# The last mixture of a graph kernel: 32 lists of one expert, or 8 lists of four

## The reference, cut to what matters

```python
    xf = x.reshape(-1, D)                       # 8192 x 128, layer-normed
    logits = xf @ router_w.T + router_b         # E = 32
    idx = jnp.argmax(logits, axis=-1)
    h = jnp.einsum('nd,ndh->nh', xf, jnp.take(W1, idx, axis=0)) + jnp.take(b1, idx, axis=0)   # H = 32
    h = jax.nn.relu(h)
    out = jnp.einsum('nh,nhd->nd', h, jnp.take(W2, idx, axis=0)) + jnp.take(b2, idx, axis=0)
    out = jax.nn.relu(out)
    ...
x = x + _L3_ffn_ref(_layernorm(x, axis=-1), ...)
```

## Time and profile before

| | us |
|---|---|
| median of three runs | 1954.38 |
| lowest and highest run | 1948.59, 1958.46 |
| span of the profiled execution | 1867.1 |
| TensorE busy | 1627.8 (87%) |
| VectorE busy | 1095.9 (59%) |
| ScalarE busy | 998.9 (53%) |
| GpSimd busy | 786.7 (42%) |

### The profile page before, as it was taken

The page is one execution under the profiler, slowest core; times in us unless marked ns, Lnnn a source line. Parts: engine busy times, 40 slices in busy tenths (PEclk is TensorE's granted clock), DMA queues, the critical chain, the costliest instruction groups (busy, mean ns, idle before and its releaser), DMA issues. The chain is left out here.

```text
span 1867.1 us, 43356 instructions
## 1 busy us (share of the span) xinstructions
PE 1627.8 (87%) x13366; PEld 1314.2 (70%) x13366; DVE 1095.9 (59%) x4199; ACT 998.9 (53%) x3116; POOL 786.7 (42%) x1358
## 2 busy tenths in 40 slices
PE   7978899988859987999998888879999888884995
PEld 5756677767759985788887566679999845553542
DVE  7933433348737777699998755523333377763552
ACT  5854444446636656666665433246666534441663
POOL 6710000014426666111111677745565434554675
PEclk9989999999969999899999799989999989995998
DMA  3200000010014420000000511122222253105331
GB/s 114 84 1 1 1 1 1 1 27 1 1 36 134 123 80 1 2 3 2 2 3 3 156 47 48 62 62 70 72 71 72 56 150 86 58 24 88 100 86 35
DMA packets 125926, 91.76 MB, mean 49 GB/s; under 512 B 23591, under 2 KB 116554, under 8 KB 125701
## 3 DMA queue, kind: packets, MB, share of 16 engines
q1 hardware_dynamic: 109110, 61.89, 12.6%
q0 software_dynamic: 13568, 25.90, 4.3%
q10 hardware_dynamic: 3024, 1.21, 0.4%
HBM read 57.71 MB, written 33.30 MB: 49 GB/s over the span
## 5 line engine op out<-in xcount | busy, mean ns | idle before, releaser
L1361 ACT ACTIVATE FEAT<-BANKS,FEAT 128x128 f32<-128x128 f32 x544 | 155.5, 368 | 82.1 <-PE BANKS L1314 82.1
L1206 POOL DMA_INDIRECT scratch_made<-FEAT x136 | 144.9, 1065 | 122.6 <-DVE FEAT L1500 119.8
L1061 ACT ACTIVATE EXP<-BANKS,NEGMAX 128x128 f32<-128x128 f32 x512 | 139.4, 383 | 59.5 <-DVE NEGMAX L1073 59.5
L440 ACT ACTIVATE gates<-BANKS,EXP 128x64 f32<-128x64 f32 x384 | 97.4, 314 | 112.6 <-PE BANKS L417 112.6
L1314 PE MATMUL BANKS<-FEAT 128*128 128x128 f32 x1088 | 145.5, 277 | 0.0
L1323 PE MATMUL BANKS<-AUX,FEAT 128*128 x1088 | 144.5, 276 | 0.4 <-ACT FEAT L1361 0.4
L417 PEld LDWEIGHTS BANKS<-AUX,EXP 128*128 128x128 f32 x768 | 95.4, 191 | 69.7 <-DVE AUX L464 69.6
L1198 POOL DMA_INDIRECT scratch_sent<-FEAT,POS x128 | 125.1, 977 | 38.3 <-issue 37.5
L990 POOL COPY EXP<-AUX 128x32 f32<-128x32 f32 x256 | 42.5, 211 | 217.8 <-PE BANKS L1036 217.8
L1314 PEld LDWEIGHTS BANKS<-FEAT 128*128 128x128 f32 x1088 | 133.9, 194 | 0.0
L1323 PEld LDWEIGHTS BANKS<-AUX,FEAT 128*128 128x128 f32 x1088 | 133.2, 193 | 0.6 <-issue 0.6
(11 more groups left out here) (367 smaller groups left out, 4196.0 us busy)
## 6 DMA issues: line engine op xcount, KB each, us to landing
EXP<-in_L_ffn_W SPq DMA_DIRECT2D x128, 128.0 KB, 2.1
FEAT<-scratch_sent SPq DMA_DIRECT2D x136, 64.5 KB
EXP<-scratch_made SPq DMA_DIRECT2D x32, 256.0 KB, 3.4
FEAT<-scratch_sent SPq DMA_DIRECT2D x96, 65.5 KB, 1.9
X<-in_x SPq DMA_DIRECT2D x16, 256.0 KB, 2.9
STAGE<-in_adj SPq DMA_DIRECT2D x16, 256.0 KB, 3.3
scratch_sent<-NONE SPq DMA_DIRECT2D x48, 65.5 KB, 3.3
scratch_sent<-FEAT,POS POOLq DMA_INDIRECT x192, 2.3
```

The source lines that it names most:

```text
L440: act.activation(gates[:, at, sp_, :], PS[2 * at + par][:, u * B:(u + 1) * B], f, bias=wr["b" + gate]).then_inc(done, 1)
L1061: last = act.activation(tile(EXS[:, par], 4 * k + n), tile(PS[j], c), ACT.Exp, bias=NEGMAX[:, par, 4 * k + n:4 * k + n + 1])
L1206: pool.indirect_dma_start(out=made2, out_offset=bass.IndirectOffsetOnAxis(ap=XI_I[:, t % R_IN, H:ROW2], axis=0), in_=YO[:, t % R_OUT, :], ...
L1361: last = act.activation(tile(HR[:, t % R_H], c), tile(PS[2 + t % 2], c), ACT.Gelu, bias=BT[:, c, t:t + 1])
```

## The change

The 32 experts are held as 8 lists of four (`L3` = 8, `M3` = 4). The list is expert // 4, and expert mod 4 travels with the token as a one-hot of four words at the front of its row (135 words instead of 131). The stream has 64 + 8 = 72 tiles, or 18 quads.

A tile now meets all four experts of its list at once. The first layer is one product over the whole array: 128 inputs to 4 x 32 hidden values. A mask product adds the bias: a one-hot column times a table `BT3` that holds b1 where expert and column agree and -2^100 elsewhere, so that relu turns the three other experts' hidden values to zero. The second layer is one product of 128 x 128 for a tile, on top of the b2 picked by the same one-hot. The one-hots of four tiles are turned by one transpose. Every stage works on a quad. There is one unread product of 256 columns a quad, where there was one a tile.

```diff
-        NT3 = B * T // P + E3
+        NT3 = B * T // P + L3
...
+                def clear(i):
+                    if i == 0:
+                        pool.memset(BT3, NEVER).then_inc(s.none, 1)
+                        pool.memset(OP3, 0.0).then_inc(s.none, 1)
+                    if i < 3:
+                        pool.memset(BR3[i], 0.0).then_inc(s.none, 1)
+                in_turn(NG, [(0, dev), (2, dev2), (2, clear), (6, send)])
...
                 def later(i):
+                    if i < L3:
+                        some = slice(M3 * i, M3 * i + M3)
+                        sp.dma_start(WT3[:, 256 * i:256 * i + P].rearrange("p (e f) -> p e f", e=M3),
+                                     a["L3_ffn_W1"][some].rearrange("e d f -> d e f")).then_inc(load_e3, 16)
+                        sp.dma_start(WT3[:, 256 * i + P:256 * i + 2 * P], a["L3_ffn_W2"][some].rearrange("e f d -> (e f) d")
+                                     ).then_inc(load_e3, 16)
...
-                for e in range(0, E3 // 2):
+                for e in range(0, L3 // 2):
                     r = sp.value_load(ZROW3[0:1, e:e + 1]).with_bounds(min_val=0, max_val=ROWS3 - P)
                     sp.dma_start(sent3[bass.ds(r, P), :], NONE3[:, e:e + ROW3]).then_inc(s.ex3_blank, 16)
...
-                in_turn(NT3, [(0, turn), (0, keep_warm), (1, up), (2, down)])
+                def turn(q):
+                    reused(pe, s.ex3_hot, q, 2)
+                    pe.wait_ge(s.ex3_xn, q + 1)
+                    pe.transpose(OB3[q % 2][:, 0:P], OP3[:, q % 2, :], ident[:])
+                    pe.matmul(OB3[q % 2][:, P:3 * P], ident[:], ident[:].unsqueeze(1).to_broadcast([P, 2, P]), start=True, stop=True)
+                    reused(pe, s.ex3_xT, q, 2)
+                    transpose4(pe, PS[q % 2], XN3[:, q % 2], s.ex3_t_ps)
+
+                def mask(q):
+                    pe.wait_ge(s.ex3_hot, q + 1)
+                    pe.wait_ge(s.ex3_w, 8 * (q + 1))
+                    reused(pe, s.ex3_hT, q, 2)
+                    reused(pe, s.ex3_y, q, 2)
+                    for j in range(4):
+                        pe.matmul(tile(PS[2 + q % 2], j), BR3[q % 3][:, j, 0:P], OT3[:, q % 2, :],
+                                  start=(j == 0), stop=False, skip_group_check=True)
+                    pe.matmul(Y3[q % 2].rearrange("p (k h) -> p k h", k=4), OT3[:, q % 2, :], BR3[q % 3][:, :, P:2 * P],
+                              start=True, stop=False, skip_group_check=True)
+
+                def up(q):
+                    pe.wait_ge(s.ex3_xT, q + 1)
+                    for j in range(4):
+                        last = pe.matmul(tile(PS[2 + q % 2], j), WR3[q % 3][:, 256 * j:256 * j + P], tile(XT3[:, q % 2], j),
+                                         start=False, stop=True, skip_group_check=True)
+                    last.then_inc(s.ex3_h_ps, 1)
+
+                def down(q):
+                    pe.wait_ge(s.ex3_hT, q + 1)
+                    for j in range(4):
+                        last = pe.matmul(tile(Y3[q % 2], j), tile(HT3[:, q % 2], j), WR3[q % 3][:, 256 * j + P:256 * j + 2 * P],
+                                         start=False, stop=True, skip_group_check=True)
+                    last.then_inc(s.ex3_y_ps, 1)
+                in_turn(NQ, [(0, turn), (1, mask), (1, up), (2, down)])
...
+                def first(q):
                     reused(act, s.ex3_y_ps, q, 3)
+                    for j in range(4):
+                        e = act.value_load(EOFI3[0:1, 4 * q + j:4 * q + j + 1]).with_bounds(min_val=0, max_val=L3 - 1)
+                        rows = slice(32 * j, 32 * j + M3)
+                        act.copy(BR3[q % 3][rows, j, :], BT3[rows, bass.ds(e * 256, 256)]).then_inc(s.ex3_w, 1)
+                        act.copy(WR3[q % 3][:, 256 * j:256 * j + 256], WT3[:, bass.ds(e * 256, 256)]).then_inc(s.ex3_w, 1)
+
+                def units(q):
+                    act.wait_ge(s.ex3_h_ps, q + 1)
+                    reused(act, s.ex3_y_ps, q, 2)
+                    act.activation(HT3[:, q % 2, :], PS[2 + q % 2], ACT.Relu).then_inc(s.ex3_hT, 1)
...
+                in_turn(NQ, [(2, units), (0, first)])
...
                     v.wait_ge(s.idx, i + 1)
+                    v.tensor_scalar(PART3[:, par, 0, :], IDX3[:].bitcast(INT32)[:, par, :, 0], 2, None, ALU.arith_shift_right)
+                    v.tensor_scalar(PART3[:, par, 1, :], IDX3[:].bitcast(INT32)[:, par, :, 0], M3 - 1, None, ALU.bitwise_and
+                                    ).then_inc(s.part, 1)
...
+                    v.tensor_tensor(OUTBOX3[:, i % R_SEND3, :, 0:M3], iota32[:, 0:M3].unsqueeze(1).to_broadcast([P, G, M3]),
+                                    PART3[:, par, 1, :].unsqueeze(2).to_broadcast([P, G, M3]), ALU.is_equal)
...
-                in_turn(NT3, [(0, norm), (1, xT), (3, result)])
+                def norm(q):
+                    reused(v, s.ex3_t_ps, q, 2)
+                    for j in range(4):
+                        t = 4 * q + j
+                        v.wait_ge(s_in3[t % R3], 16 * (t // R3 + 1))
+                        v.tensor_scalar(tile(XN3[:, q % 2], j), XI3[:, t % R3, AT_X:AT_R], XI3[:, t % R3, AT_R:AT_R + 1],
+                                               XI3[:, t % R3, AT_R + 1:AT_R + 2], ALU.mult, ALU.add)
+                    at = 4 * q % R3
+                    v.tensor_copy(OP3[:, q % 2, :].rearrange("p (k c) -> p k c", k=4)[:, :, 0:M3], XI3[:, at:at + 4, 0:M3]).then_inc(s.ex3_xn, 1)
+
+                def xT(q):
+                    v.wait_ge(s.ex3_t_ps, q + 1)
+                    reused(v, s.ex3_h_ps, q, 2)
+                    v.tensor_copy(OT3[:, q % 2, :], OB3[q % 2][:, 0:P]).then_inc(s.ex3_hot, 1)
+                    v.tensor_copy(XT3[:, q % 2, :], PS[q % 2]).then_inc(s.ex3_xT, 1)
...
+                in_turn(NQ, [(4, result), (2, xT), (0, norm)])
```

More of the change, by code:

```diff
@@ L32 @@
 SPARSITY = 0.01
+NEVER = -2.0 ** 100
 CAPACITY = float(-(-B * T * 5 // (4 * E1)))
@@ new lines, in program @@
+        OT3 = EXP[:, 2048:2048 + 2 * P].rearrange("p (a n) -> p a n", a=2)
+        OP3 = EXP[:, 3072:3072 + 2 * P].rearrange("p (a n) -> p a n", a=2)
+        WT3 = AUX[:, 0:L3 * 256]
+        BT3 = AUX[:, L3 * 256:2 * L3 * 256]
+        BT3_G = BT3.rearrange("p (g n) -> p g n", g=L3)
+        WR3 = [w[:].rearrange("p a n -> p (a n)") for w in (WA, WB, WF)]
+        BR3 = [AUX[:, 4096 + 1024 * k:5120 + 1024 * k].rearrange("p (k n) -> p k n", k=4) for k in range(3)]
+        LE3, PRP3 = (EXP[:, 4200 + 40 * k:4200 + 40 * k + L3] for k in range(2))
@@ L1645, in later @@
                     if i == 0:
-                        sp.dma_start(b1_3[:], a["L3_ffn_b1"]).then_inc(load_e3, 16)
-                        sp.dma_start(W1_3.rearrange("p (e f) -> p e f", e=E3), a["L3_ffn_W1"].rearrange("e d f -> d e f")
-                                     ).then_inc(load_e3, 16)
                         sp.wait_ge(s.ctab, 3)
-                    if i >= 1 and i < 9:
-                        for k in range(4 * (i - 1), 4 * i):
-                            sp.dma_start(sent3[E3 * CAP3 + k * P:E3 * CAP3 + (k + 1) * P, :], NONE3[:, E3 + k:E3 + k + ROW3]
-                                         ).then_inc(s.blank, 16)
@@ L1654, in later @@
-                    if i == 9:
-                        sp.dma_start(W2R3.rearrange("p (e d) -> p e d", e=E3), a["L3_ffn_W2"].rearrange("e f d -> f e d")).then_inc(s.ex3_w2, 16)
-                        sp.dma_start(B2R3, a["L3_ffn_b2"].rearrange("(o e) d -> o (e d)", o=1)).then_inc(s.ex3_w2, 16)
+                    if i >= 1 and i < 1 + L3:
+                        k = i - 1
+                        sp.dma_start(sent3[L3 * CAP3 + k * P:L3 * CAP3 + (k + 1) * P, :], NONE3[:, L3 + k:L3 + k + ROW3]
+                                     ).then_inc(s.blank, 16)
@@ new lines, in later @@
+                    if i >= 9 and i < 9 + 4:
+                        sp.wait_ge(s.none, 1)
+                        j = 32 * (i - 9)
+                        for e in range(M3):
+                            sp.dma_start(BT3_G[j + e:j + e + 1, :, F3 * e:F3 * e + F3],
+                                         a["L3_ffn_b1"].rearrange("(g e) f -> e g f", e=M3)[e:e + 1]).then_inc(load_e3, 16)
+                        sp.dma_start(BT3_G[j:j + M3, :, P:2 * P], a["L3_ffn_b2"].rearrange("(g e) d -> e g d", e=M3)).then_inc(load_e3, 16)
@@ L1657, in _ @@
                 in_turn(NG, [(0, fetch), (2, later)])
-                sp.wait_ge(s.blank, 1 + E3 * 16)
+                sp.wait_ge(s.blank, 1 + L3 * 16)
                 def load(t):
@@ L1754, in _ @@
                 pe.transpose(PS[5][0:1, 256:256 + NT3], ROWF3[0:NT3, :], ident[0:NT3, 0:NT3]).then_inc(s.ex3_flip, 1)
-                pe.wait_ge(s.ex3_oneh, 1)
-                for j in range(4):
-                    last = pe.matmul(PS[6][F3 * j:F3 * (j + 1), 0:NQ], b1_3[:],
-                                     ONEH3.rearrange("p (q j) -> p j q", j=4)[:, j, :], start=True, stop=True)
-                last.then_inc(s.ex3_bb, 1)
```

(25 more changed lines are left out.)

169 lines of the change are left out of this document (57 added, 112 removed), and 8 rows, old and new, of the table s.

## The result

The changed kernel took 1899.8 us, the median of four runs (1892.88 to 1909.53), beside 1955.4 for the kernel before: a ratio of 0.9716, interval 0.9677 to 0.9756. It is faster by 55.6 us where 32.7 were forecast, and 1899.8 lies under the range.

What follows compares the result with a forecast made beforehand. GpSimd's result scatter, 1.286 us a tile, was taken to bound the last expert stream. On the profiled span of 1867.1 us, the median's 87.3 more left as is, -30.9 - 10.1 + 8.3 - 0.5 + 0.5 = -32.7: 1921.7 us, range 1908 to 1938.

Steps and rivals of the forecast that it cites:

- Tiles: Last expert stream: 96 tiles become 72 at the scatter's pace of 1.286 us a tile, -30.9 us.
- TensorE: Expert stream: TensorE's time for four tiles at full clock, 4.9 to 5.6 us, 5.1 likeliest.
- By a hair: Expert stream: the scatter's 5.14 us for four tiles holds the pace just ahead of TensorE's 5.1.
- The rival of a TensorE bound: Expert stream: TensorE sets the pace at 5.6 us a quad, 1929.4 us in all; chance 0.23.
- the serial handshake: Expert stream: mask waits for VectorE's copy each time, 6.4 us a quad, 1943 us in all; chance 0.08.
- The low-clock rival: Expert stream: TensorE's clock stays at 1.2 GHz, 9 us a quad, 1987 us in all; chance 0.05.
- Gap: Between last list scatter and first expert load: loads start at 1708.9 instead of 1718.96, -10.1 us.
- the earlier scatter: End of the last routing loop: the last list scatter is issued at 1706.5, -1.0 us.
- The blanks: Before the expert loads: 32 blank tiles become 8, their issues end near 1700, then the last list scatter sets the end.
- Fill: From first load to first result scatter of the expert stream: 20.9 us against 12.6, +8.3 us.
- Routing loop: Last layer's routing loop: narrower rank products save 0 to 2 us, taken as -0.5.
- The clears on GpSimd: First three routing groups: 5 us of clears, from 0 if hidden to +5 uncovered, taken as +0.5.

Runs made afterwards that it cites:

- the stores: Changed kernel with the last stage's indirect result scatters replaced by plain stores of whole tiles to consecutive rows, late session: 1878.8 us, ratio 0.9528 to the kernel before.

## Why the prediction was wrong

*The failed step* is the first sentence of the sum: the median "lies 87.3 above it; no view shows that part and I leave it as it is". A term of 87.3 us was put at no change, with no other reason than that no view shows it. The description of the kernel before says of it that the run times are longer by what lies around the span, and that is wrong too: it lies inside the span of the executions that were timed, and the change takes some 22 us of it away. Of the kernel before's 105 us more in the session with traces of both (spans 1970.1 and 1865.4), 54 are there when the last layer starts (1547 against 1494 us; 41 of them in the scatters of the layer before, 12 right behind these) and 50 come in the expert stream, the very stretch whose tiles are removed. The forecast of -32.7 was one for a quiet kernel, and there -29.7 was measured. In a late session each removed tile is worth 1.72 us instead of 1.284, about 10 us over 24, and the new form leaves out 12.7 more. The way of the change and its main step, fewer tiles at the scatter's pace, were right.

*Tiles.* -30.9 forecast, -30.9 in the quiet traces, 24 x 1.284. That the scatter keeps the pace held: 1.2 us of waits for VectorE in 85.

*TensorE.* Estimated 4.89 bare, 5.1 with waits, 5.6 for the rival; the stores show 4.78. "By a hair" was 0.35 us a quad. The rival of a TensorE bound is out, and the serial handshake too, since either would hold the stores at 5.6 us a quad or more. The low-clock rival is out: the clock is 0.95 in the quiet stream, and without the unread product a late session gave no other time. (The bound of that rival, 17 x 7.1 + 3.9, is 124.6 and not 124.4, which changes nothing.) The Trainium skill, "TensorEngine Tiling (Array Packing)", Performance Considerations, favours four row tiles for a contraction of 32, which speaks against the change. The 96 tiles in the new form, with the old form's 122.0 us for 95 intervals, show that giving them up costs nothing while another engine has the pace.

*Gap.* -10.1 forecast with the earlier scatter, -5.9 measured. The blanks were what filled it, as forecast, and the last scatter follows the loop's last group sooner by 1.5; but the loop itself ended 3.7 later, which is inside the -5.9, and the loads start 3.0 us after the last scatter rather than 2.4.

*Fill.* +8.3 forecast, +7.9 measured, with the granted clock at 0.50 and 0.64 up to 1726.

*Routing loop.* -0.5 forecast, +3.7 measured: mis-sized, with the wrong sign. I priced the rank products at their durations, and did not ask what TensorE's clock does when it has less to do. The clears on GpSimd, put at +0.5, don't show: the first list scatter starts at 1552.1 against 1552.5 before.

That the quiet gain came within 3 us of the forecast is in part luck: 3.0 us too little at the last list scatter and 1.2 in the wait behind it stand against 1.4 at the end that nothing in the sum had.

## What to carry to other kernels

Before a sum is made, hold the profiled span against the timed runs: if they differ by more than a few us, take a span of the executions that were timed, and look for the stretch in which the rest lies. Where a stretch is full of indirect scatters, removing some may be worth more than their quiet pace, as in four sessions here. Slack between dependent steps may be worth more than a short fill. Taking work from TensorE was not free: it cost 3.7 us of a loop that the work was hidden in.

## What the hardware showed that was not expected

- With an indirect scatter every 1.28 us, what waits for TensorE started late in the late sessions (2.8 us in the stretch shown), and SyncE's register instructions took up to 717 ns instead of 29; with plain stores on the same queue in their place neither occurred. In quiet sessions the same program shows next to nothing of it.
- The two stretches of scatters that pay are those with 1.28 and 1.39 us from one to the next on average in a quiet session. Two others are spared: the result scatters of the layer before (136, 1.9 us apart: 256.4 us from first to last in a late session against 255.0) and the last routing loop (64, 2.5 us apart: 157.1 against 156.2). That fits a price that comes with frequent scatters, but no run changed their distance. What makes a session late stays open.
- The chip is known of five sessions; the three late ones and the two quiet ones ran on five different chips, so whether it is the chip or the hour can't be told.
- A plain store of 128 rows occupies GpSimd 0.54 us, an indirect one 0.98. The Trainium skill, "Perfetto Trace Analysis", DMA Instruction — SWDGE (GPSIMD), says that this time is the making of descriptors and not the moving of data. The trace agrees as far as it goes: the list scatters land 2.5 us after issue in the median, long after their 0.96 us.
- The old form paid 0.53 us a tile for the lateness, the new one 0.39 in the same session. The old one signals between engines for each tile, the new one mostly for each quad. A rival is TensorE's clock: in that session it is granted 0.82 in the old stream and 0.94 in the new, where quiet ones have 0.97 and 0.95. Neither was tested.
